# A Mamba block's scan loop and its output projection: C products in buffers of their own by state, last decays moved, a second projection group split, two low tiles on GpSimd

## The chip, the core and the metric

One core of one Trainium2 chip runs the whole program. The metric is the device time of one execution in microseconds (us); a run of this program has a median of 373.48 us over three runs (373.43 to 373.91). A core has TensorE (PE, matrix products; its weight loads are PEld), VectorE (DVE), ScalarE (ACT), GpSimd (POOL) and SyncE (SP, which here only issues DMAs). All of them run their own queue of instructions in order and wait for one another by semaphores.

## The reference, cut to what matters

Six blocks follow one another on x, 2 x 64 rows of 1024 values, each as x = x + block(layernorm(x)): a quantised product with a context, a Mamba block, a mixture of low-rank experts, a cross attention, a self attention with rotary positions, and a permuted MLP. The change lies in the second, where D = 2048 channels and N = 16 states:

```python
def step(state, xs):
    d_t, B_t, C_t, u_t = xs
    dA = jnp.exp(d_t[..., None] * A)
    state = dA * state + (d_t * u_t)[..., None] * B_t[:, None, :]
    y_t = jnp.einsum('bdn,bn->bd', state, C_t)
    return (state, y_t)
...
y = jnp.swapaxes(ys, 0, 1) + u * D_param
y = y * jax.nn.silu(gate)
return y @ W_out.T
```

## The kernel before

Time and batch (2 x 64 = 128) lie on the free axis, channels on the 128 partitions: 16 channel tiles k of 128. The 16 states are handled as two halves of 8 (HN), so the scan has 32 steps (STEPS): step s is channel tile s // 2, state half s % 2, a tile of 128 x 1024 values in the order (batch, state, time). Four steps make a quad (QUAD), which is two channel tiles; its y is gathered in one PSUM bank, y_bank(q). Every engine runs its own list of the steps, written out by hand:

- ScalarE: decay(s) (line 793, eight Exp of 128 x 126) makes dA; three buffers, so decay(s) waits for the scan of s - 3. In between stand the softplus parts, copies of the projection, the tanh of a gate group (gate_tanh, line 730), and DMA issues.
- TensorE: scan_input(s) (line 1138) puts the input of the scan into two PSUM banks; state_sum(s) (line 1180) sums the products over the states by accumulating transposes; fold_y(q) (line 1190) turns the sum back to channels on partitions and adds the two halves of a column block (ident2 is two identities on top of one another); turn (line 959) and gate tiles of W_in (line 1063) lie between. In iteration s of the loop at line 1193 the order is scan_input(s), turns, gate tile, state_sum(s - 3), fold.
- VectorE: scan(s) (line 1671) is one tensor_tensor_scan; then silu of a gate group (line 1609), copy_y(q) (line 1684, the y bank to h), skip_y(q) (line 1691, u * D added).
- GpSimd: the product of the state with C, in place (line 630), for steps 0 to 30; step 31 is on VectorE (times_c, line 1677). gate_y (line 621) multiplies a quad by its gate.

A state is in one of STATES = 4 buffers; scan(s) waits until state_sum(s - 4) has read that buffer.

Behind the loop comes the output projection, y @ W_out.T: 16 channel tiles in four groups (GD = 4 tiles), two halves nh of 512 output columns, eight units of W_out (1 MB each). Groups 0 and 1 are plain float32 products (output, line 1215, two passes for each). Groups 2 and 3 (GATE_HALF = 2 on) are split: ScalarE rounds unit m (high(m), line 820) and the left side (gated_high, line 810), VectorE takes the differences (low(m), line 1727; gated_low, line 1705), and split_products (lines 1002 and 1009) makes three products for each tile. There are three buffers for split units, so high(m) waits for the end of unit m - 3; two of the three lie over the scan's own buffers. gated_high(2) stands in ScalarE's loop at s = 30, between decays 30 and 31, since its left side needs the gate of quad 5, which GpSimd does behind product 30. The end of the projection is y_psum, 1 and 2: add_to_x (line 1482) adds the block's result to x, and the next block begins.

Weights come through a ring of 7 slots in the order of unit_list(). SP issues unit n when the unit before it in its slot is used up (last_use): for a split unit that is its low(m), for a plain one the product that reads it last. One slot more (x_wq 1) waits for y_psum 2.

## Time and profile before

| | |
|---|---|
| median of three runs | 373.48 us (373.43 to 373.91) |
| the profiled execution | 374.15 us, of which span 372.4 us |
| TensorE busy | 336.3 us (90%) |
| VectorE busy | 267.0 us (72%) |
| ScalarE busy | 206.0 us (55%) |
| GpSimd busy | 107.7 us (29%) |
| scan loop | about 84 to 184 us |
| mean granted TensorE clock | 0.989 |

The span is the time from the first to the last instruction; what is left of the execution's time lies around it. The granted clock is given as a share of TensorE's full speed. In a timeline a row is one instruction or several of the same kind back to back; its start counts from the start of the span, and what stands in brackets is how long the engine was idle before it and what ended that. Matmuls are pipelined: a row's length holds the tail of its last one, so the distance between the starts of two rows is the better measure of work.

### The profile page before, as it was taken

What the parts mean: (1) busy time and instruction counts of PE and PEld (TensorE: products, weight loads), DVE (VectorE), ACT (ScalarE), POOL (GpSimd) and SP (SyncE); (2) the same over time, 40 slices, a digit from 0 to 9 for tenths busy, and PEclk for the clock granted to TensorE, in tenths of its full rate; (3) what the DMA queues carried; (4) which work ended last, traced back from release to release, by engine and by line L of the source; (5) the groups of instructions that cost most, each with busy time, mean ns of one, the idle gap of its engine ahead of it and who ended that gap; (6) DMA issues with size and microseconds to landing.
All of it is one profiled execution on the core that took longest, in us unless ns stands there. A gap on an engine that the chain in (4) does not pass through costs nothing.

```text
span 372.4 us, 5061 instructions
## 1 busy us (share of the span) xinstructions
PE 336.3 (90%) x1928; PEld 215.4 (58%) x1928; DVE 267.0 (72%) x362; ACT 206.0 (55%) x402; POOL 107.7 (29%) x75
## 2 busy tenths in 40 slices
PE   0688999999899999999499999899999999899996
PEld 0334664653555555555165776687343577787795
DVE  2877887647979989886556698995721798975381
ACT  1985633189999999880702774463022468350350
POOL 2501000026988988888000020202000020300000
PEclk9999999999999999999699999999999999999999
DMA  6999999753030020661147799589999995000001
GB/s 243 423 422 419 420 325 422 283 212 113 2 110 6 0 113 3 225 243 46 57 127 271 285 396 400 215 329 352 393 429 363 427 422 236 2 2 2 0 2 56
DMA packets 12966, 81.85 MB, mean 220 GB/s; under 512 B 2109, under 2 KB 2365, under 8 KB 3661
## 3 DMA queue, kind: packets, MB, share of 16 engines
q1 hardware_dynamic: 11614, 78.23, 53.9%
q10 hardware_dynamic: 1296, 3.22, 2.3%
q8 instruction: 15, 0.25, 0.2%
q14 instruction: 9, 0.07, 0.1%
q0 software_dynamic: 32, 0.07, 0.1%
HBM read 80.86 MB, written 0.52 MB: 219 GB/s over the span
## 4 chain that ended last, share of the span: by engine, by line
PE 66%; DVE 17%; ACT 7%; DMA 6%; issue 2%; POOL 1%; SPq 0%; DVEq 0%; ACTq 0%
PE psum L1063 11%; PE psum L1002 8%; PE psum L1295 7%; PE psum L1138 7%; PE psum L1180 6%; DMA ring<-in_ctx 6%; PE psum L1215 4%; PE psum L1009 4%; PE psum L959 3%; DVE rounded L1727 3%; ACT arena L793 3%; PE psum L1414 2%; PE psum L1449 2%; PE psum L1190 2%; DVE arena L1671 2%
## 5 line engine op out<-in xcount | busy, mean ns | idle before, releaser
L793 ACT ACTIVATE arena<-arena 128x126 f32<-128x126 f32 x256 | 76.6, 394 | 3.2 <-DVE arena L1671 2.9
L1671 DVE TENSOR_TENSOR_SCAN arena<-arena,psum 128x1024 f32<-128x1024 f32 x24 | 54.6, 2281 | 5.8 <-PE psum L1138 5.0
L630 POOL TENSOR_TENSOR arena<-arena 128x1024 f32<-128x1024 f32 x23 | 54.3, 2365 | 8.4 <-DVE arena L1671 8.4
L571 POOL TENSOR_TENSOR small<-small 128x1 f32<-128x1 f32 x6 | 9.6, 1608 | 144.2 <-DVE small L1498 138.6
L1063 PE MATMUL psum<-ring,hT 128*128 128x512 f32 x104 | 50.2, 605 | 0.8 <-ACT hT L694 0.8
L1727 DVE TENSOR_TENSOR rounded<-ring,rounded 128x2048 fp32r<-128x2048 f32 x16 | 36.5, 2286 | 15.9 <-ACT rounded L820 15.9
L820 ACT ACTIVATE rounded<-ring 128x2048 fp32r<-128x2048 f32 x16 | 30.5, 1913 | 17.8 <-PE psum L1009 10.5
L1138 PE MATMUL psum<-plain 64*128 64x512 f32 x128 | 36.1, 641 | 0.4 <-DVE plain L1671 0.3
L1063 PEld LDWEIGHTS psum<-ring,hT 128*128 128x128 f32 x104 | 17.8, 190 | 21.9 <-issue 20.8
L1180 PEld LDWEIGHTS psum<-ident,arena 128*128 128x128 f32 x192 | 22.0, 141 | 11.7 <-issue 9.7
L1002 PE MATMUL psum<-rounded,split 128*128 128x512 f32 x96 | 24.7, 399 | 2.4 <-DVE rounded L1727 1.8
L1180 PE MATMUL psum<-ident,arena 128*128 128x128 f32 x192 | 25.2, 274 | 0.0
L1295 PE MATMUL psum<-ring,arena 128*64 128x512 f32 x96 | 24.4, 593 | 0.0
L1215 PE MATMUL psum<-ring,arena 128*128 128x512 f32 x32 | 16.9, 679 | 6.0 <-DVE arena L1609 6.0
L959 PE MATMUL psum<-ident,arena 128*128 128x128 f32 x120 | 18.7, 280 | 3.9 <-DVE arena L1649 1.5
L630 POOL TENSOR_TENSOR plain<-plain,arena 128x1024 f32<-128x1024 f32 x8 | 18.9, 2369 | 10.7 <-DVE plain L1671 10.7
L1002 PEld LDWEIGHTS psum<-rounded,split 128*128 128x128 f32 x96 | 17.5, 188 | 7.5 <-DVE rounded L1727 2.9
L959 PEld LDWEIGHTS psum<-ident,arena 128*128 128x128 f32 x120 | 13.4, 140 | 14.4 <-issue 8.7
L683 ACT ACTIVATE arena<-ring,small 128x2048 uint8<-128x2048 f32 (+1 forms) x9 | 16.9, 1900 | 7.9 <-DMA ring<-in_ctx 7.9
L959 PE MATMUL psum<-ident,h 128*128 128x128 f32 x48 | 7.4, 304 | 15.1 <-DVE h L1509 11.7
L1671 DVE TENSOR_TENSOR_SCAN plain<-arena,psum 128x1024 f32<-128x1024 f32 x8 | 18.2, 2277 | 2.5 <-PE psum L1138 2.4
L820 ACT ACTIVATE arena_halves<-ring 128x2048 fp32r<-128x2048 f32 x8 | 15.3, 1917 | 6.2 <-PE psum L1009 5.6
(237 smaller groups left out, 595.3 us busy)
## 6 DMA issues: line engine op xcount, KB each, us to landing
ring<-in_w_in SPq DMA_DIRECT2D x16, 1024.0 KB, 15.2
ring<-in_ctx SPq DMA_DIRECT2D x13, 1024.0 KB, 10.8
ring<-in_w_out SPq DMA_DIRECT2D x8, 1024.0 KB, 4.8
ring<-in_ctx_t SPq DMA_DIRECT2D x7, 1024.0 KB, 5.9
ring<-in_w_base SPq DMA_DIRECT2D x4, 1024.0 KB, 4.9
ring<-in_x_wk SPq DMA_DIRECT2D x4, 1024.0 KB, 9.8
ring<-in_a_wo SPq DMA_DIRECT2D x4, 1024.0 KB, 11.5
ring<-in_x_wq SPq DMA_DIRECT2D x3, 1024.0 KB, 9.0
```

What stands on the lines that cost most here:

```text
L630: pool.tensor_tensor(state[s % STATES], state[s % STATES], c, ALU.mult).then_inc(product_ready, 1)
L793: last = act.activation(to, of, ACT.Exp, scale=a_par[:, k, state_no:state_no + 1])
L820: act.activation(unit_halves[m % 3][:, 0, :, :], slot(split_units[m]), ACT.Copy).then_inc(unit_high, 1)
L959: last = pe.transpose(psum[:, bank, P * k:P * k + P], tile[:, c:c + P], ident[:, :])
L1002: pe.matmul(psum[:, bank, :], left(0, k0 + k), unit[:, w, k, :], start=(start and k == 0 and w == 0), stop=False)
L1063: last = pe.matmul(psum[:, proj_bank(j), :], hT[:, k, :], slot(w_in + u)[:, k % UK, :], **at)
L1138: last = pe.matmul(psum[:, input_bank(s, b), :], du[rows_of(b), left], bdiag[rows_of(b), right, :], start=True, stop=True)
L1180: last = pe.matmul(psum[:, y_bank(q), to:to + P], state[s % STATES][:, of:of + P], ident[:, :], start=(s % 2 == 0 and b == 0 and n == 0), ...
L1215: last = pe.matmul(psum[:, 4 + nh, :], sg[:, k, :], slot(u)[:, k % GD, :], start=(k == 0), stop=False)
L1295: last = pe.matmul(psum[L * b:L * b + L, bank, :], left[:, UK * kh + k, L * b:L * b + L], slot(u0 + b)[:, k, :], start=(kh == 0 and k == 0 ...
L1671: dve.tensor_tensor_scan(state[s % STATES], dA[:, s % 3, :], psum[:, p:p + 2, :].rearrange("p a b -> p (a b)"), 0.0, ALU.mult, ALU.add).th ...
L1727: dve.tensor_tensor(unit[:, 1, :, :], slot(split_units[m]), unit[:, 0, :, :].bitcast(F32), ALU.subtract).then_inc(unit_low, 1)
```

## The change

- state and product are apart: STATES = 3 state buffers and three product buffers. The product is written in the order (state, batch, time). scan(s) waits for the product of s - 3, the product of s waits for state_sum(s - 3).
- state_sum transposes 128 columns, one state of both batches, eight per step as before, all into the same 128 columns of y_bank; copy_y copies 256 columns, fold_y is two transposes.
- On ScalarE gated_high(2) is taken out of the loop, the last gate_tanh comes ahead of decay(31), and the load of bk goes behind product 30, because its place is now a state buffer.
- GATE_HALF = 1: group 1 of the output projection is split too. The low tiles of groups 1 and 2 are GpSimd's (behind its products), that of group 3 stays with VectorE. The order of W_out's units and all later numbers of split units (up by two) follow. On VectorE low(0) now comes first behind the loop.

```diff
-STATES = 4
+STATES = 3
-GATE_HALF = 2
+GATE_HALF = 1
-    units += [("w_out", i) for i in (0, 4, 1, 5, 2, 3, 6, 7)]
+    units += [("w_out", i) for i in (0, 4, 1, 2, 3, 5, 6, 7)]
...
-        state = [plain[:, 3 * HN * P:4 * HN * P]] + [carve(arena, 13408 + HN * P * i, HN * P) for i in range(STATES - 1)]
+        state = [carve(arena, 19040, HN * P), carve(arena, 23296, HN * P), plain[:, 3 * HN * P:4 * HN * P]]
+        product = [carve(arena, 13408 + HN * P * i, HN * P) for i in range(STATES)]
...
-        uses(None, None)
         for nh in range(2):
-            uses(None, (y_psum, nh + 1), split=True)
+            uses(None, None, (y_psum, nh + 1), split=True)
...
-                pool.tensor_tensor(state[s % STATES], state[s % STATES], c, ALU.mult).then_inc(product_ready, 1)
+                if s >= STATES:
+                    pool.wait_ge(reduced, s - STATES + 1)
+                pool.tensor_tensor(product[s % STATES].rearrange("p (n b t) -> p b n t", n=HN, b=B),
+                                   state[s % STATES].rearrange("p (b n t) -> p b n t", b=B, n=HN),
+                                   c.rearrange("p (b n t) -> p b n t", b=B, n=HN), ALU.mult).then_inc(product_ready, 1)
...
+            for g in range(GATE_HALF, 3):
+                pool.wait_ge(sg_high_ready, g - GATE_HALF + 1)
+                v = slice(GD * g, GD * g + GD)
+                pool.tensor_tensor(sg_low[:, v, :], sg[:, v, :], sg_high[:, v, :].bitcast(F32), ALU.subtract).then_inc(
+                    sg_low_ready, 1)
...
             for s in range(3, STEPS):
+                if s - 1 == GATE_AT[-1]:
+                    gate_tanh(NG - 1)
                 decay(s)
...
-                if s - 1 in GATE_AT:
+                if s - 1 in GATE_AT[:-1]:
                     gate_tanh(GATE_AT.index(s - 1))
...
-                if s == 30:
-                    gated_high(GATE_HALF)
...
-                    act.dma_start(bk, dram["bk"].to_broadcast([P, D])).then_inc(bias_in, 16)
...
             high(0)
+            gated_high(1)
+            gated_high(2)
...
             act.wait_ge(dbu_ready, STEPS)
-            act.wait_ge(reduced, STEPS - STATES + 1)
+            act.wait_ge(product_ready, STEPS - 1)
+            act.dma_start(bk, dram["bk"].to_broadcast([P, D])).then_inc(bias_in, 16)
             high(1)
+            act.wait_ge(reduced, STEPS)
+            high(2)
             gated_high(3)
-            for m in range(2, 7):
+            for m in range(3, 9):
                 high(m)
...
-                for b in range(B):
-                    to = 2 * P * (s // 2 % 2) + P * b
-                    for n in range(HN // 2):
-                        of = P * HN // 2 * b + P * n
-                        last = pe.matmul(psum[:, y_bank(q), to:to + P], state[s % STATES][:, of:of + P], ident[:, :],
-                                         start=(s % 2 == 0 and b == 0 and n == 0), stop=(s % 2 == 1 and n == HN // 2 - 1),
-                                         is_transpose=True, skip_group_check=True)
+                to = P * (s // 2 % 2)
+                for n in range(HN):
+                    last = pe.matmul(psum[:, y_bank(q), to:to + P], product[s % STATES][:, P * n:P * n + P], ident[:, :],
+                                     start=(s % 2 == 0 and n == 0), stop=(s % 2 == 1 and n == HN - 1), is_transpose=True,
+                                     skip_group_check=True)
...
-                for n in range(2 * B):
+                for n in range(2):
                     of = UN * (q % 2) + P * n
-                    last = pe.matmul(psum[:, y_bank(q), L * n:L * n + L], h[:, of:of + P], ident2, start=True, stop=True)
+                    last = pe.transpose(psum[:, y_bank(q), P * n:P * n + P], h[:, of:of + P], ident[:, :])
...
             for nh in range(2):
-                for k in range(GD, 2 * GD):
-                    output(nh, k)
-            for nh in range(2):
                 for g in range(GATE_HALF, NG):
...
-                    split_products(4 + nh, lambda a, k: (sg_low if a else sg_high)[:, k, :], 2 * nh + g - GATE_HALF, GD * g,
+                    split_products(4 + nh, lambda a, k: (sg_low if a else sg_high)[:, k, :], 3 * nh + g - GATE_HALF, GD * g,
...
                 if s >= STATES:
-                    dve.wait_ge(reduced, s - STATES + 1)
+                    dve.wait_ge(product_ready, s - STATES + 1)
...
-                dve.tensor_copy(h[:, UN * (q % 2):UN * (q % 2) + UN], psum[:, y_bank(q), :]).then_inc(y_copied, 1)
+                dve.tensor_copy(h[:, UN * (q % 2):UN * (q % 2) + 2 * P], psum[:, y_bank(q), 0:2 * P]).then_inc(y_copied, 1)
...
+            low(0)
             skip_y(STEPS // QUAD - 2)
             gate_y(STEPS // QUAD - 2)
-            gated_low(GATE_HALF)
+            low(1)
             copy_y(STEPS // QUAD - 1)
-            low(0)
             skip_y(STEPS // QUAD - 1)
             gate_y(STEPS // QUAD - 1)
-            low(1)
+            low(2)
             gated_low(3)
-            low(2)
-            low(3)
-            low(4)
+            for m in range(3, 7):
+                low(m)
```

## Rows read from the trace of the kernel before

**Rows 1.** Windows: us, busy us of each engine, granted clock, DMA share, GB/s.

```profile
125.00:150.00 25.00, 25.00 (x137) 14.64 (x138) 22.78 (x19) 23.93 (x80) 22.21 (x12) 1.00 0.12 43
...
180.00:185.00 5.00, 3.02 (x4) 1.50 (x5) 3.82 (x3) 4.72 (x6) 0.00 (x0) 0.50 0.26 103
...
235.00:240.00 5.00, 4.75 (x21) 3.86 (x21) 4.93 (x9) 2.29 (x3) 0.52 (x1) 1.00 0.26 79
```

**Rows 2.** TensorE's timeline in the loop: start us, length us, line, operation, count.

```profile
131.32 1.04 PE L1180 MATMUL psum<-ident,arena 128*128 128x128 f32 x8
132.19 1.00 PE L1190 MATMUL psum<-arena,h 128*128 128x64 f32 x8
133.13 1.13 PE L1138 MATMUL psum<-plain 64*128 64x512 f32 x4
```

**Rows 3.** Waits of VectorE from 96 to 175: us in total, times, longest.

```profile
DVE arena L1671 <- PE psum L1138: 5.0, 7, 1.2
```

**Rows 4.** GpSimd by line and form: count, busy us, mean ns of one.

```profile
L630 POOL TENSOR_TENSOR arena<-arena 128x1024 f32<-128x1024 f32 x23 | 54.3, 2365 | 8.4 <-DVE arena L1671 8.4
...
L653 POOL TENSOR_TENSOR arena<-arena,small 128x512 f32<-128x512 f32 x4 | 4.2, 1045 | 20.1 <-DVE small L1896 20.1
L614 POOL TENSOR_TENSOR arena<-arena 128x512 f32<-128x512 f32 x3 | 3.9, 1285 | 0.1
L594 POOL TENSOR_SCALAR x<-x,small 128x1024 f32<-128x1024 f32 x1 | 3.1, 3079 | 0.1
```

**Rows 5.** GpSimd's timeline behind product 30.

```profile
176.92 0.73 POOL L621 TENSOR_TENSOR arena<-arena 128x256 f32<-128x256 f32 x1
```

**Rows 6.** ScalarE's timeline at the loop's end, [idle before it, what ended that].

```profile
166.02 2.44 ACT L793 ACTIVATE arena<-arena 128x126 f32<-128x126 f32 x8
177.68 0.63 ACT L810 ACTIVATE arena_halves<-arena 128x512 fp32r<-128x512 f32 x1 [9.22 <-POOL arena L621]
...
180.54 0.57 ACT L730 ACTIVATE arena<-psum 128x512 f32<-128x512 f32 x1
181.01 1.90 ACT L820 ACTIVATE rounded<-ring 128x2048 fp32r<-128x2048 f32 x1
```

**Rows 7.** VectorE's timeline, one row of the loop, the others about its end.

```profile
130.26 0.67 DVE L1684 COPY h<-psum 128x512 f32<-128x512 f32 x1
...
172.25 2.28 DVE L1671 TENSOR_TENSOR_SCAN arena<-arena,psum 128x1024 f32<-128x1024 f32 x1
181.15 0.69 DVE L1609 SCALAR_TENSOR_TENSOR arena<-arena,psum 128x512 f32<-128x512 f32 x1 [6.61 <-ACT arena L730]
181.75 2.28 DVE L1671 TENSOR_TENSOR_SCAN arena<-arena,psum 128x1024 f32<-128x1024 f32 x1
184.06 1.23 DVE L1677 TENSOR_TENSOR arena<-arena 128x1024 f32<-128x1024 f32 x1
...
188.09 0.61 DVE L1691 SCALAR_TENSOR_TENSOR arena<-arena,small,psum 128x128 f32<-128x128 f32 x2 [2.20 <-PE psum L1190]
188.73 0.42 DVE L1699 TENSOR_TENSOR arena<-arena 128x256 f32<-128x256 f32 x1
```

**Rows 8.** TensorE's timeline, the first output products (three k tiles).

```profile
181.98 5.24 PE L1215 MATMUL psum<-ring,arena 128*128 128x512 f32 x6 [6.03 <-DVE arena L1609]
```

**Rows 9.** The chain that ended last: start us, length us, what, count.

```profile
194.94 6.92 PE psum L1215 x16
201.86 1.86 PE psum L1002 x8
203.72 0.93 PE psum L1009 x4
```

**Rows 10.** GpSimd's timeline, two of its one-element operations.

```profile
220.21 2.52 POOL L571 TENSOR_TENSOR small<-small 128x1 f32<-128x1 f32 x1 [42.56 <-DVE small L1498]
...
348.09 0.55 POOL L571 TENSOR_TENSOR small<-small 128x1 f32<-128x1 f32 x1 [21.68 <-DVE small L1498]
```

**Rows 11.** VectorE's timeline at the first of these two.

```profile
220.05 4.48 DVE L1727 TENSOR_TENSOR rounded<-ring,rounded 128x2048 fp32r<-128x2048 f32 x2
```

More of the change, by code:

```diff
@@ L1758, in _ @@
             center()
-            low_part(5, 0)
+            low_part(7, 0)
             left_low(2)
-            low_part(5, 1)
+            low_part(7, 1)
             variance(2)
-            low(6)
-            low(7)
+            low(8)
+            low(9)
             dve.wait_ge(bias_in, 48)
@@ L1787, in _ @@
                               ALU.mult).then_inc(g_ready, 1)
-            low(8)
+            low(10)
             dve.wait_ge(biased, 2)
@@ L1795, in _ @@
             center()
-            low_part(9, 0)
+            low_part(11, 0)
             left_low(4)
-            low_part(9, 1)
+            low_part(11, 1)
             variance(3)
-            low(10)
-            low(11)
+            low(12)
+            low(13)
             def query(nh):
@@ L1816, in _ @@
             query(0)
-            low(12)
+            low(14)
             query_low(0)
             query(1)
-            low(13)
-            low(14)
+            low(15)
+            low(16)
             query_low(1)
-            low(15)
+            low(17)
             dve.wait_ge(xk_psum, 2)
@@ L1847, in _ @@
                 if nh == 0:
-                    low(16)
+                    low(18)
                 dve.wait_ge(xatt_psum, nh + 1)
@@ L1853, in _ @@
             center()
-            low_part(17, 0)
+            low_part(19, 0)
             left_low(6)
-            low_part(17, 1)
+            low_part(19, 1)
             variance(4)
-            low(18)
+            low(20)
             step(dve.memset(vdup.rearrange("p b (h d) -> p (b h) d", d=DH + 1)[:, :, DH:], 1.0))
@@ L1871, in rotate @@
                 dve.tensor_tensor(to.rearrange("p (h d) -> p h d", h=heads), c, s, ALU.add).then_inc(signal, 1)
-            low(19)
+            low(21)
             dve.wait_ge(tables_in, 16)
@@ L1879, in _ @@
                 if n:
-                    low(21)
+                    low(23)
+                    low(24)
+                else:
                     low(22)
-                else:
-                    low(20)
                 dve.wait_ge(aq_psum, n + 1)
@@ L1887, in _ @@
                 rotate(psum[:, 7 if n else 1, :], H // 2, qrot[:, halves(n)], qrot_ready)
-            low(23)
+            low(25)
             dve.wait_ge(rstd_ready, 5)
@@ L1925, in _ @@
             divide(1)
-            low(24)
+            low(26)
             attn_low(1)
-            low(25)
+            low(27)
             for nh in range(2):
```

73 lines of the change are left out of this document (39 added, 34 removed).

## Prediction

> **What bounds the kernel now.** I read the windows first. Inside the scan loop TensorE is busy in all of 125 to 150 us, VectorE for 22.78 and ScalarE for 23.93 of the 25 [rows 1]. So I took TensorE's timeline over a few steps. Each step s issues the scan's input (line 1138, four matmuls), eight accumulating transposes of a product (line 1180) and mostly one gate tile; each fourth step also folds y (line 1190). The starts stand directly behind one another, so the engine's own work sets the pace: eight transposes take 0.87 us, and from a fold's start to the next input it is 0.94 [rows 2]. VectorE agrees: between 96 and 175 us its scans waited seven times, 5.0 us together, for that input, from scan 13 on; the longest, 1.2 us, is scan 17's [rows 3].
>
> Then the end of the loop. Scan 30 starts at 172.25, scan 31 only at 181.75 [rows 7]. Why: ScalarE did decays 30 at 166.02 (2.44 us), then stood 9.22 us in gated_high(2) [rows 6], which needs the gate that GpSimd does behind product 30, 0.73 us at 176.92 [rows 5]; only then came decays 31 and, at 180.54, the last tanh. The last silu, at 181.15 [rows 7], is what the first output product waited for: TensorE stood from 175.95 to 181.98, 6.03 us [rows 8], and came back at a granted clock of 0.50 [rows 1], which is the 1.2 GHz level; later it is at 2.4 GHz again. From there to about 213.1 (the end of the output projection: four split units of 1.86 + 0.93 = 2.8 us each from 201.86 on [rows 9]) TensorE has no gap. Everything later hangs on that moment.
>
> **The change part by part.** All times are on the old trace's axis.
>
> 1. *Products summed whole.* The state lies in the order (batch, state, time), the product now (state, batch, time), so that one transpose handles all 128 columns of one state. state_sum still has eight transposes: nothing saved. But y fills 256 columns instead of 512, and a fold is two transposes instead of eight passes. Price of two: at 0.87/8 each 0.22, and I take 0.28 for the start-up of so short a group. Saving 0.94 - 0.28 = 0.66 us per fold [rows 2]. copy_y halves too, from 0.67 to about 0.40 on VectorE [rows 7].
> How much of it counts? Not the fold of step 8: scan 9 waits for a tanh there. Of those of steps 12, 16, 20, 24 and 28 all do, if TensorE stays last. At step 17 two folds make it 1.32 earlier, against VectorE's 1.2 of waiting and about 0.7 that it gains itself (two half copies and a small wait): TensorE is still last. The 5.0 us of waiting and five half copies of 0.27 are more than five folds of 0.66. Sum 5 x 0.66 = 3.3; for friction with VectorE I take 3.2. ScalarE may run decays up to three steps ahead. Bounds: 0 (another engine takes over at once) and 3.3 + 0.7.
>
> 2. *New waits.* A scan waits for the product three steps back instead of the sum four back; a product waits for the sum three back. Queued behind a waiting scan are silu, copy_y and the next scan, behind a waiting product GpSimd's gates, and TensorE's sums wait for those. A product takes 2.365 [rows 4] and a step about 2.9, so the product three back is over some 3 us before it is needed. The sum three back ends before the scan of its step does (the input plus at most a gate tile and eight transposes, about 2.1 us, against the input plus a scan of 2.29). Margin 0.2 us or more: 0. If that margin goes, the product starts late by the difference, once a step.
>
> 3. *GpSimd's product with a permuted write.* No row shows one. The nearest: 128x512 with a broadcast operand in runs of 64 took 1.045 us, contiguous 1.285, so a three-dimensional read is not dearer; and upwards, the dearest 1024 columns of the engine, 3.08 for the scalar addition to x [rows 4]. I take 2.37 as before, the row nearest in kind. GpSimd then has 4 x 2.37 + 0.73 = 10.2 us per quad, where a quad of the new loop takes about 11.1: up to 2.6 us a product costs nothing, and cheaper is worth nothing.
>
> 4. *Last decays ahead.* gated_high(2) leaves the loop and the last tanh goes before decays 31. The turn that the tanh reads is queued on TensorE directly behind the input of scan 30, so it ends near 172; tanh 0.57 [rows 6], end near 172.7; decays 2.4, end near 175.0. Silu follows scan 30 at 174.5, 0.69; scan 31 runs from 175.1 to 177.4, its product of 1.23 to 178.7 [rows 7], the half copy to 179.1. What is late next for TensorE is the sum of product 29 (it ended before 174.6, and the sum of 28 is ahead of it): until 175.9, where TensorE's gap began. So output(0, 0) starts at 175.9 instead of 181.98: **6.1 us**. Without the gap I expect the full clock: the six passes of the first three products took 5.24 [rows 8], sixteen later ones 6.92 [rows 9], so six cost 2.6, and with 0.1 for the tail of the last this saves **2.5**. But fold 6 follows at 178.5 and needs the half copy of 179.1 and its semaphore: **0.7 lost**. The two last folds save 2 x 0.66 = **1.3**.
>
> 5. *Group 1 split.* Eight k tiles: 6.92 us plain, against two units of 2.8 [rows 9]: **1.3 saved**. Added are two ScalarE roundings of 1.90 [rows 6] and two VectorE differences of 2.24 (two took 4.48, [rows 11]). Covered? Fold 7 needs copy_y(7), now queued behind low(0), skip, gate and low(1): 179.1 + 2.25 + 0.6 + 0.4 [rows 7] + 2.25 = 184.6, with the copy 185.1. TensorE reaches that fold at 185.5: covered by 0.4. The six units then end at 188.5, 191.3, 194.1, 196.9, 199.7 and 202.5. A rounding waits for the end of the unit three before, and rounding and difference, 4.2 us, stand beside two units of 5.6: covered by 1.4. For the third unit skip, gate, low(2) and gated_low(3) end near 189.8, against 191.3: covered. Where this cover goes, each microsecond of VectorE is one of the total.
>
> 6. *Two low tiles on GpSimd*, 1.285 each [rows 4], ready near 179 and 180.5 and needed at 185.7 and 188.5. What they meet matters. GpSimd's one-element operation took 0.55 us at 348.09 but 2.52 at 220.21 [rows 10], where VectorE had begun a difference of two SBUF tensors 0.16 us earlier [rows 11]; it ended just behind that difference. So GpSimd is held by such VectorE work. Whether VectorE is held in turn no row shows: bounds 0 and all of the GpSimd work that meets it. If it is, VectorE's product of step 31 waits 0.2 for GpSimd's gate, low(0) about 1.0 for the first low tile, gate_y(6) 0.7 for the second; copy_y(7) ends near 187 and TensorE waits **1.5**. I take this value, since the hold seen lasted a whole instruction and most likely works both ways.
> The Trainium skill (SBUF — State Buffer, Who interferes with whom) states this lock for both directions; on the one that a row shows, the trace agrees with its 2.52 us. By that page the sum holds the 1.5, without it the sum is 1.5 more.
>
> 7. *DMA and queues.* The load of bk moves behind product 30 on ScalarE's queue, because its place is now a state buffer; its reader stands behind the two differences of 220.05 [rows 11], over 30 us later. SP's order of w_out follows the new use; the last one still waits for output(0, 3). The w_base loads wait for low tiles that come earlier. All later loads wait for releases that move with the work; at 235 to 240 the DMA engines had a share of 0.26 [rows 1], so the dense loading behind it is not backed up and moves too: 0.
>
> Sum: 3.2 + 6.1 + 2.5 - 0.7 + 1.3 + 1.3 = 13.7, less 1.5 for the hold: **12.2 us**. The profiled execution took 374.15 (span 372.4), so 361.95; the median of the runs, 373.48, lies 0.67 below it, which gives 361.3.
>
> **The rivals.**
> - *VectorE is not held by GpSimd:* 13.7 gained, 359.8. For: no row shows it held. Against: GpSimd is.
> - *The loop does not speed up*, because ScalarE (23.93 of 25 us) or VectorE is last as soon as TensorE gains: 3.2 less, 364.5. Against: VectorE's waits for inputs.
> - *The gain is given back downstream*, transfers becoming last behind 240 us. For: the dense loading there; against: the idle stretch before it. Half of the 12.2, about 367.4.
> - *The change does not do what it says:* scan 31 still late, say by a tanh held by its turn. Then loop, folds and split alone: 3.2 + 1.3 + 1.3 = 5.8, about 367.7.
> - *Slower: GpSimd's permuted product is dear.* It costs from 2.6 us on. A quad of 11.75 us now becomes 4X + 0.73; over six quads the tail's gain of 9 is gone at X = 3.1, just above the dearest row. At 3.3 the loop loses 13.1, and the time is about 377.5. For: nothing but the missing row.
> The Trainium skill (GPSIMD Engine Reference, Performance pitfalls for Q7 kernels) charges about half more for reads with an inner step over 8 bytes. The inner step stays at 4 bytes here, so by the page there is no charge; no row shows the charged case.
>
> **How the numbers follow.** Forecast 361.3 with 0.44; VectorE not held 0.27; loop not faster 0.14; downstream 0.05; change without effect 0.05; slower 0.03; and 0.02 for no change at all. The range of 359.0 to 365.0 takes in the first three, 0.85, with the 0.7 more that the loop may give. A measurement of this kernel tells 0.2% (0.75 us) from no change. Faster 0.95, same 0.02, slower 0.03.
>
> **What would show it.** Folds of two transposes, and some 11.1 us from fold to fold; scan 31 right behind the silu, near 172; no 6 us gap on TensorE and a granted clock of 1.00 throughout; the product at 2.37; VectorE's low(0) longer than 2.24 or late behind its copy, if the hold is real; the output projection's end near 201 instead of 213; the rest moved by one amount. I am wrong if the product takes over 2.6, if TensorE waits over 2 us for fold 7, or if the stretch behind the projection grows.

## The result, and the profile after

The changed kernel takes 361.20 us (median of four runs, 361.14 to 361.25) against 373.70 for the kernel before on the same chip (four runs, 373.43 to 374.41): a ratio of 0.9663, with a 95% interval of 0.9646 to 0.9679. The forecast was 361.3, its range 359.0 to 365.0. Of all the executions behind the medians of this document one is left out, the profiled one of the kernel without GpSimd's low tiles: it took 1129.9 us, where its four others took 360.6 to 360.7.

| | before | after |
|---|---|---|
| the profiled execution | 374.15 us | 361.25 us |
| its span | 372.4 us | 359.4 us |
| TensorE / VectorE busy | 336.3 / 267.0 us | 327.7 / 269.8 us |
| ScalarE / GpSimd busy | 206.0 / 107.7 us | 210.3 / 112.9 us |
| end of the output projection | 212.89 | 199.96 |
| from there to the end of the span | 159.5 | 159.4 |

The last two rows say where the gain lies: all 12.9 us of it ahead of the next block, and nothing given back behind. (The end is read at TensorE's idle products that follow the projection: line 965 before, line 979 after.)

The changed kernel's granted clock over the span in 40 slices, in tenths of full speed (9 stands for 90% or more):

```profile
PEclk9999999999999999999999999999999999999999
```

Windows of the changed kernel (us, busy us of PE, PEld, DVE, ACT and POOL, granted clock, DMA share, GB/s), to be held against [rows 1]:

```profile
125.00:150.00 25.00, 25.00 (x134) 13.85 (x133) 23.07 (x20) 24.90 (x84) 23.36 (x13) 1.00 0.16 53
180.00:185.00 5.00, 4.58 (x21) 2.94 (x20) 4.43 (x7) 2.45 (x2) 0.01 (x1) 1.00 0.71 256
```

In the loop TensorE is still full, and VectorE (23.07) and ScalarE (24.90) came nearer to it; ScalarE is now busy in all but 0.1 us of these 25. Behind the loop the granted clock is 1.00 where it was 0.50.

TensorE's timeline (start us, length us, line; idle time before it and what ended that), to be held against [rows 2] and [rows 8]:

```profile
130.65 1.04 PE L1192 MATMUL psum<-ident,arena 128*128 128x128 f32 x8
131.53 0.38 PE L1202 MATMUL psum<-ident,h 128*128 128x128 f32 x2
131.84 1.13 PE L1152 MATMUL psum<-plain 64*128 64x512 f32 x4
...
172.63 2.74 PE L1227 MATMUL psum<-ring,arena 128*128 128x512 f32 x6
175.99 0.44 PE L1202 MATMUL psum<-ident,h 128*128 128x128 f32 x2 [0.61 <-DVE h L1696]
...
182.89 0.44 PE L1202 MATMUL psum<-ident,h 128*128 128x128 f32 x2 [0.42 <-DVE h L1696]
183.08 2.11 PE L1016 MATMUL psum<-rounded,arena_halves 128*128 128x512 f32 x8
...
199.96 1.05 PE L979 MATMUL psum<-ident 128*128 128x128 f32 x8
```

A fold (now line 1202) takes 0.31 us from its start to the next input, instead of 0.94. The first output products start at 172.63, directly behind the sums, and six passes take 2.74 instead of 5.24. Two short waits are left, 0.61 and 0.42, each ahead of a fold, and each for VectorE's copy of y.

ScalarE's timeline, decays 31, to be held against [rows 6]:

```profile
169.50 2.42 ACT L803 ACTIVATE arena<-arena 128x126 f32<-128x126 f32 x8
```

VectorE's timeline over the end of the loop, to be held against [rows 7]:

```profile
169.10 2.28 DVE L1680 TENSOR_TENSOR_SCAN arena<-arena,psum 128x1024 f32<-128x1024 f32 x1
171.30 0.66 DVE L1618 SCALAR_TENSOR_TENSOR arena<-arena,psum 128x512 f32<-128x512 f32 x1
171.96 2.29 DVE L1680 TENSOR_TENSOR_SCAN arena<-arena,psum 128x1024 f32<-128x1024 f32 x1
174.28 1.32 DVE L1687 TENSOR_TENSOR arena<-arena 128x1024 f32<-128x1024 f32 x1
175.52 0.41 DVE L1696 COPY h<-psum 128x256 f32<-128x256 f32 x1
175.86 3.03 DVE L1741 TENSOR_TENSOR rounded<-ring,rounded 128x2048 fp32r<-128x2048 f32 x1
...
179.44 0.86 DVE L1712 TENSOR_TENSOR arena<-arena 128x256 f32<-128x256 f32 x1
180.22 2.28 DVE L1741 TENSOR_TENSOR rounded<-ring,rounded 128x2048 fp32r<-128x2048 f32 x1
```

Scan 30 starts at 169.10, which is 3.15 earlier than before, and scan 31 directly behind the last silu, at 171.96. Then two rows are longer than their work: low(0) at 175.86 (3.03, the next one of the same form 2.28) and gate_y(6) at 179.44 (0.86, against 0.42 in [rows 7]). GpSimd is what they meet. Its rows by line and form, and its timeline there:

```profile
L632 POOL TENSOR_TENSOR arena<-arena 128x1024 f32<-128x1024 f32 x21 | 49.4, 2361 | 15.0 <-DVE arena L1680 14.8
...
L645 POOL TENSOR_TENSOR arena_halves<-arena,arena_halves 128x512 fp32r<-128x512 f32 x2 | 5.5, 2786 | 0.0
```

```profile
174.48 5.53 POOL L645 TENSOR_TENSOR arena_halves<-arena,arena_halves 128x512 fp32r<-128x512 f32 x2
```

The product with its permuted write (line 632) costs 2.361 on average, against 2.365 contiguous [rows 4]. The two low tiles (line 645) took 5.53 together, where two contiguous subtractions or products of this size take 2 x 1.285 [rows 4]. Put in a row, the numbers fit two engines that let each other pass one instruction at a time: tile 1 waits for product 31, low(0) for tile 1, tile 2 for low(0), and gate_y(6) for tile 2, which ends at 180.01.

### The profile page after: what moved, and what is told of

Same layout as the page of the kernel before. It is cut to its first block, busy times and chain, and to the rows that moved or that the text cites. A ratio compares the mean times of both kernels' runs of the same rounds, so it can differ in the third digit from the quotient of the medians.

```text
span 359.4 us, 5024 instructions
## 1 busy us (share of the span) xinstructions
PE 327.7 (91%) x1888; PEld 210.1 (58%) x1888; DVE 269.8 (75%) x363; ACT 210.3 (59%) x405; POOL 112.9 (31%) x77
## 4 chain that ended last, share of the span: by engine, by line
PE 58%; DVE 20%; ACT 11%; DMA 6%; issue 3%; POOL 0%; SPq 0%; DVEq 0%; ACTq 0%
PE psum L1077 11%; PE psum L1016 9%; PE psum L1304 8%; DMA ring<-in_ctx 6%; ACT arena L803 6%; PE psum L1152 5%; PE psum L1023 5%; PE psum L1192 4%; PE psum L973 3%; DVE rounded L1741 3%; DVE arena L1680 2%; PE psum L1423 2%; PE psum L1458 2%; DVE arena_halves L1741 2%; DVE rounded L1749 1%
## 5 line engine op out<-in xcount | busy, mean ns | idle before, releaser
L632 POOL TENSOR_TENSOR arena<-arena 128x1024 f32<-128x1024 f32 x21 | 49.4, 2361 | 15.0 <-DVE arena L1680 14.8
L1680 DVE TENSOR_TENSOR_SCAN arena<-arena,psum 128x1024 f32<-128x1024 f32 x22 | 49.9, 2278 | 4.8 <-PE psum L1152 3.1
L830 ACT ACTIVATE rounded<-ring 128x2048 fp32r<-128x2048 f32 x18 | 34.5, 1917 | 20.0 <-PE psum L1023 10.4
L1192 PEld LDWEIGHTS psum<-ident,arena 128*128 128x128 f32 x256 | 28.9, 141 | 16.8 <-issue 14.8
L1192 PE MATMUL psum<-ident,arena 128*128 128x128 f32 x256 | 33.6, 275 | 0.0
L1016 PE MATMUL psum<-rounded,split 128*128 128x512 f32 x104 | 26.6, 398 | 1.4 <-ACT split L701 0.7
L1680 DVE TENSOR_TENSOR_SCAN plain<-arena,psum 128x1024 f32<-128x1024 f32 x10 | 22.8, 2278 | 1.6 <-PE psum L1152 1.3
L632 POOL TENSOR_TENSOR arena<-plain,arena 128x1024 f32<-128x1024 f32 x10 | 23.6, 2359 | 1.3 <-DVE plain L1680 1.2
L973 PE MATMUL psum<-ident,arena 128*128 128x128 f32 x120 | 18.7, 280 | 4.5 <-DVE arena L1658 1.5
L1016 PEld LDWEIGHTS psum<-rounded,split 128*128 128x128 f32 x104 | 19.0, 188 | 6.4 <-ACT split L701 1.7
L973 PEld LDWEIGHTS psum<-ident,arena 128*128 128x128 f32 x120 | 13.4, 140 | 14.9 <-issue 9.3
L973 PE MATMUL psum<-ident,h 128*128 128x128 f32 x48 | 7.4, 304 | 15.0 <-DVE h L1518 11.6
L1741 DVE TENSOR_TENSOR arena_halves<-ring,arena_halves 128x2048 fp32r<-128x2048 f32 x8 | 18.3, 2285 | 0.8 <-ACT arena_halves L830 0.8
## 6 DMA issues: line engine op xcount, KB each, us to landing
ring<-in_a_wo SPq DMA_DIRECT2D x4, 1024.0 KB, 11.6
```

Of the source, the lines that this page charges most:

```text
L632: pool.tensor_tensor(product[s % STATES].rearrange("p (n b t) -> p b n t", n=HN, b=B), state[s % STATES].rearrange("p (b n t) -> p b n t", ...
L830: act.activation(unit_halves[m % 3][:, 0, :, :], slot(split_units[m]), ACT.Copy).then_inc(unit_high, 1)
L973: last = pe.transpose(psum[:, bank, P * k:P * k + P], tile[:, c:c + P], ident[:, :])
L1016: pe.matmul(psum[:, bank, :], left(0, k0 + k), unit[:, w, k, :], start=(start and k == 0 and w == 0), stop=False)
L1192: last = pe.matmul(psum[:, y_bank(q), to:to + P], product[s % STATES][:, P * n:P * n + P], ident[:, :], start=(s % 2 == 0 and n == 0), sto ...
L1680: dve.tensor_tensor_scan(state[s % STATES], dA[:, s % 3, :], psum[:, p:p + 2, :].rearrange("p a b -> p (a b)"), 0.0, ALU.mult, ALU.add).th ...
```

## The experiments

The theory was the prediction's sum: products by state, the decays moved ahead and the split are three gains that add, because TensorE is last everywhere, less a hold of VectorE by GpSimd. All times are medians; "saved" is against the kernel before as it was measured beside each. Those medians lie between 373.70 and 374.18, so a difference of some 0.3 us between two changed kernels is no more than that scatter, unless rows show where it arises; the ratios, which take the scatter out in part, are given for this.

### Do the parts add?

Decays ahead alone. The last tanh goes ahead of decays 31, gated_high(2) behind high(0); gate_y on VectorE waits for GpSimd's gate before it, and the rest is the kernel before.

```diff
             for s in range(3, STEPS):
+                if s - 1 == GATE_AT[-1]:
+                    gate_tanh(NG - 1)
                 decay(s)
...
-                if s - 1 in GATE_AT:
+                if s - 1 in GATE_AT[:-1]:
...
-                if s == 30:
-                    gated_high(GATE_HALF)
...
             high(0)
+            gated_high(GATE_HALF)
```

> The kernel before with one part of the change: gated_high(2) behind high(0), the last tanh ahead of decays 31, and VectorE's gate waiting for GpSimd's. Theory A (my sum): the 6.0 us gap of TensorE and the 2.5 us of slow clock go, and fold 6 then waits some 1.0 us for a full copy_y(6); 7.5 us saved, 366.2. Rival B: the clock falls elsewhere, or the gap only moves to another wait; 6 saved or less, 367.7 and up.

Measured: 366.60 us (366.55 to 366.67), ratio 0.9809 (0.9794 to 0.9823), 7.3 saved. TensorE's timeline of it:

```profile
175.75 2.74 PE L1216 MATMUL psum<-ring,arena 128*128 128x512 f32 x6
179.38 1.10 PE L1191 MATMUL psum<-arena,h 128*128 128x64 f32 x8 [0.89 <-DVE h L1685]
```

Output(0, 0) follows the sums at 175.75, within 0.2 of the 175.9 that the prediction read from the place where the gap began. The six passes run at once in 2.74. Fold 6 waits 0.89, since the copy of y is still a whole bank here.

Products by state alone. Three state and three product buffers, the sums, copies and folds of the changed kernel, and the load of bk moved, as the buffers need; decays, projection and units as before.

```diff
-STATES = 4
+STATES = 3
...
-                pool.tensor_tensor(state[s % STATES], state[s % STATES], c, ALU.mult).then_inc(product_ready, 1)
+                if s >= STATES:
+                    pool.wait_ge(reduced, s - STATES + 1)
+                pool.tensor_tensor(product[s % STATES].rearrange("p (n b t) -> p b n t", n=HN, b=B),
...
-                for n in range(2 * B):
+                for n in range(2):
                     of = UN * (q % 2) + P * n
-                    last = pe.matmul(psum[:, y_bank(q), L * n:L * n + L], h[:, of:of + P], ident2, start=True, stop=True)
+                    last = pe.transpose(psum[:, y_bank(q), P * n:P * n + P], h[:, of:of + P], ident[:, :])
```

> The kernel before with the other part: products by state in own buffers, half copies, folds of two transposes (the load of bk moved, which the buffers need). Theory A: 3.15 us in the loop and 2 x 0.63 for the last two folds, scan 31 still stalled by decays 31 as before: 4.4 saved, 369.3. Rival B: the fold's saving is hidden behind other engines when alone, or the stall takes it; 373.7.

Measured: 369.71 us (369.44 to 370.22), ratio 0.9893 (0.9878 to 0.9908), 4.2 saved. TensorE's timeline of it:

```profile
178.87 5.35 PE L1219 MATMUL psum<-ring,arena 128*128 128x512 f32 x6 [6.03 <-DVE arena L1613]
```

The whole block of work came 3.1 earlier (178.87 against 181.98), and the gap of 6.03 with the slow passes behind it (5.35) is untouched. The loop's gain and the gap are two separate things.

Both, without the split: GATE_HALF and the order of the units stay as before, and the low tile of group 2 stays with VectorE.

> Both parts together, group 1 of the projection plain and the low tile of group 2 on VectorE as before. Theory A: the parts add, and the changed kernel has only 1.3 for the split units less 0.4 for the wait of fold 7 on top: 362.0 to 362.1. Rival B: the split and GpSimd's tiles bring the whole 1.3, 362.5. Rival C: they bring nothing, 361.2.

Measured: 361.95 us (361.85 to 361.96), ratio 0.9683 (0.9667 to 0.9699), 12.0 saved. Singly the two saved 7.3 + 4.2 = 11.5. They add, and 0.3 of what is over is the shorter wait of fold 6. TensorE's timeline of it, the two folds behind the loop:

```profile
176.05 0.44 PE L1195 MATMUL psum<-ident,h 128*128 128x128 f32 x2 [0.62 <-DVE h L1692]
...
182.37 0.38 PE L1195 MATMUL psum<-ident,h 128*128 128x128 f32 x2
```

Here fold 7 has no wait. So of the changed kernel's 361.20 the split accounts for 0.75 only: its own 1.3, less about 0.6 for the wait of fold 7 that came with it.

The changed kernel with the decays' part undone: the tanh behind decays 31, gated_high(1) and (2) between decays 30 and 31.

```diff
-                if s - 1 == GATE_AT[-1]:
-                    gate_tanh(NG - 1)
                 decay(s)
...
-                if s - 1 in GATE_AT[:-1]:
+                if s - 1 in GATE_AT:
...
+                if s == 30:
+                    gated_high(1)
+                    gated_high(2)
...
             high(0)
-            gated_high(1)
-            gated_high(2)
```

> The changed kernel with the decays part undone: gated_high(1) and (2) in the loop at s = 30, the last tanh behind decays 31. Theory A: TensorE's gap of 6 us and the slow clock come back (6.1 + 2.5), while the waits of fold 6 (0.6) and fold 7 (0.4) go: 368.8. Rival B: the decays part is worth only the gap, 366.3 to 367.

Measured: 368.25 us (367.78 to 368.62), ratio 0.9852 (0.9836 to 0.9868), 7.05 more than the changed kernel, where the same part alone saved 7.3. Its windows and TensorE's row behind the gap:

```profile
180.00:185.00 5.00, 5.00 (x18) 2.68 (x17) 4.96 (x6) 1.91 (x1) 0.00 (x0) 0.75 0.56 196
```

```profile
178.87 4.59 PE L1226 MATMUL psum<-ring,arena 128*128 128x512 f32 x6 [6.04 <-DVE arena L1617]
```

The gap is back (6.04), and with it a granted clock of 0.75 in 180 to 185. Here the six passes took 4.59, not 5.24: what the clock costs behind the gap varied between 1.9 and 2.6 us in the three kernels that have it (passes of 4.59, 5.24 and 5.35, at a mean granted clock of 0.60, 0.52 and 0.50, against 2.74).

### Does GpSimd hold VectorE, and what does it cost?

The question is whether the two take turns, in both directions, when both read two operands from SBUF, or only GpSimd waits. First the price in this kernel. GpSimd's low tiles are taken away; ScalarE writes them as zeros instead, so the low part of two groups is missing from the product.

```diff
-            for g in range(GATE_HALF, 3):
-                pool.wait_ge(sg_high_ready, g - GATE_HALF + 1)
...
             high(1)
+            act.wait_ge(sg_high_ready, 2)
+            for g in range(GATE_HALF, 3):
+                v = slice(GD * g, GD * g + GD)
+                act.activation(sg_low[:, v, :], sg[:, v, :], ACT.Copy, scale=0.0).then_inc(sg_low_ready, 1)
```

> The changed kernel without GpSimd's two low tiles: ScalarE writes zeros in their place while it is idle behind high(1), so the low part of groups 1 and 2 is left out of the result. Theory A: VectorE's low(0), product 31 and gate_y(6) return to 2.28, 1.23 and 0.42, and only the 0.42 us that TensorE waited for fold 7 counts: 360.8. Rival B: the hold costs the 1.5 of the prediction: 359.7. Rival C: the longer VectorE instructions have another cause than GpSimd: they stay, 361.2.

Measured: 360.65 us (four runs, 360.58 to 360.67), ratio 0.9642 (0.9628 to 0.9656): 0.55 below the changed kernel by the medians, 0.8 by the ratios. No rows of this kernel are used, so only its times speak. The hold costs 0.55 to 0.8 us: more than the 0.4 of the expectation's theory A, but nearer to it than to the 1.5 of its rival B, and rival C (nothing) is out.

The mechanism by itself: four stages appended behind the end of the changed kernel, with four 128 x 1024 additions on each engine. Stage 1: first GpSimd alone, then VectorE alone. Stage 2: both at once. Stage 3: both at once, VectorE's second operand in PSUM. Stage 4: VectorE as in stage 2, GpSimd only writes (memset).

```diff
+                for n in range(4):
+                    last = dve.tensor_tensor(ring[:, 2 + n // 2, D * (n % 2):D * (n % 2) + D], left, right, ALU.add)
...
+                for n in range(4):
+                    to = ring[:, 4 + n // 2, D * (n % 2):D * (n % 2) + D]
+                    last = pool.memset(to, 0.0) if only_write else pool.tensor_tensor(to, left, right, ALU.add)
```

> The changed kernel with four stages behind its last addition, each of four 128x1024 additions on an engine: GpSimd alone, VectorE alone (two SBUF inputs), both at once, GpSimd with VectorE reading PSUM as the second input, and GpSimd only writing (memset) with VectorE reading two SBUF tensors. Theory A (each holds the other for whole instructions): alone 1.22 (VectorE) and about 2.36 (GpSimd); together a pair takes 3.6 and both look longer. Rival B (only GpSimd is held): VectorE stays at 1.22, GpSimd starts after VectorE's four. Rival C: both are slowed a little, by shared reading. By all of them PSUM as second input and the memset change nothing.

Measured: 400.64 us with the four stages, in a single execution. VectorE's timeline, stages 1 to 4, then the first two instructions of stage 2 singly, then GpSimd's:

```profile
366.36 4.63 DVE L2001 TENSOR_TENSOR ring<-ring 128x1024 f32<-128x1024 f32 x4 [9.34 <-POOL ring L674]
371.19 11.06 DVE L2001 TENSOR_TENSOR ring<-ring 128x1024 f32<-128x1024 f32 x4 [0.20 <-POOL small L678]
384.48 4.62 DVE L2001 TENSOR_TENSOR ring<-ring,psum 128x1024 f32<-128x1024 f32 x4 [2.23 <-POOL ring L674]
393.91 4.63 DVE L2001 TENSOR_TENSOR ring<-ring 128x1024 f32<-128x1024 f32 x4 [4.82 <-POOL ring L674]
```

```profile
371.19 1.22 DVE L2001 TENSOR_TENSOR ring<-ring 128x1024 f32<-128x1024 f32 x1 [0.20 <-POOL small L678]
372.33 3.36 DVE L2001 TENSOR_TENSOR ring<-ring 128x1024 f32<-128x1024 f32 x1
```

```profile
357.09 9.23 POOL L674 TENSOR_TENSOR ring<-ring 128x1024 f32<-128x1024 f32 x4 [21.38 <-DVE small L2003]
...
371.30 13.15 POOL L674 TENSOR_TENSOR ring<-ring 128x1024 f32<-128x1024 f32 x4
384.61 9.27 POOL L674 TENSOR_TENSOR ring<-ring 128x1024 f32<-128x1024 f32 x4 [0.17 <-POOL ring L674]
```

Alone the four take 4.63 on VectorE (1.16 each) and 9.23 on GpSimd (2.31 each). Together they took 11.06 and 13.15. If each lets the other pass after every instruction, with VectorE first, VectorE ends after 4 x 1.16 + 3 x 2.31 = 11.6 and GpSimd after 4.63 + 9.23 = 13.9: measured 11.1 and 13.3 from the first start. So both are held. The single rows show the turns themselves: VectorE's first addition takes 1.22, and each of the other three 3.35 or 3.36, its own work and one addition of GpSimd. Had the two shared the reading evenly, VectorE would have ended after some 9.3 (an estimate, twice 4.63). With one operand in PSUM nobody is held (4.62 and 9.27), nor is VectorE by a memset (stage 4: 4.63). That is the expectation's theory A. It fits the loop, where the scans, which read PSUM, took 2.28 beside GpSimd's products throughout.

The Trainium skill (SBUF — State Buffer, Who interferes with whom) states the lock for both directions; the stage with both at once agrees, with 13.3 us against 13.9 for one after the other.

The kernel with the late decays shows the same from the other side. There the same two tiles ran while VectorE stood idle (171.42 to 178.03) and took 2.50 together instead of 5.53, and low(0), which came after them, took 2.28:

```profile
174.49 2.50 POOL L645 TENSOR_TENSOR arena_halves<-arena,arena_halves 128x512 fp32r<-128x512 f32 x2
```

Is the help of GpSimd worth anything then? The low tiles of groups 1 and 2 go to VectorE, behind low(0) and low(1):

```diff
             low(0)
+            gated_low(1)
             skip_y(STEPS // QUAD - 2)
             gate_y(STEPS // QUAD - 2)
             low(1)
+            gated_low(2)
             copy_y(STEPS // QUAD - 1)
```

> The changed kernel with the two low tiles of groups 1 and 2 on VectorE (0.68 each, ahead of copy_y(7)) instead of GpSimd. Theory A: GpSimd's help is worth almost nothing, since it lengthens VectorE's work by 1.2 us where the tiles themselves take 1.36: 361.3 to 361.5. Rival B: GpSimd's tiles are free, so this costs the whole 1.36: 362.5.

Measured: 361.52 us (five runs, 361.36 to 361.55), ratio 0.9665 (0.9650 to 0.9679). VectorE's timeline:

```profile
175.92 2.28 DVE L1734 TENSOR_TENSOR rounded<-ring,rounded 128x2048 fp32r<-128x2048 f32 x1
178.12 0.68 DVE L1712 TENSOR_TENSOR arena_halves<-arena,arena_halves 128x512 fp32r<-128x512 f32 x1
```

low(0) is back at 2.28, which shows that GpSimd's tiles were what lengthened it, but VectorE does two tiles of 0.68 itself. (Product 31 still takes 1.33: that 0.1 comes from GpSimd's gate ahead of it, 173.86 to 174.58, and not from the tiles.) That is 1.36 of its own work against 1.2 of being held, and fold 7 waits 0.44 against 0.42. The two low tiles on GpSimd are worth 0.3 us by the medians and nothing by the ratios.

### What is left of the waits

The waits for folds 6 and 7 come from the order on VectorE (the copy of y behind product 31, or behind low(1)). Copy_y(6) goes ahead of scan 31, copy_y(7) behind low(0), and on TensorE the last sum directly behind the one before, fold 7 two products earlier:

```diff
             state_sum(STEPS - 2)
+            state_sum(STEPS - 1)
             output(0, 3)
             output(1, 0)
             output(1, 1)
-            state_sum(STEPS - 1)
+            fold_y(STEPS // QUAD - 1)
             output(1, 2)
             output(1, 3)
-            fold_y(STEPS // QUAD - 1)
...
+                if s == STEPS - 2:
+                    copy_y(STEPS // QUAD - 2)
...
             low(0)
+            copy_y(STEPS // QUAD - 1)
             skip_y(STEPS // QUAD - 2)
             gate_y(STEPS // QUAD - 2)
             low(1)
-            copy_y(STEPS // QUAD - 1)
```

> The changed kernel with copy_y(6) ahead of scan 31, the last state sum directly behind the one before, copy_y(7) directly behind low(0), and fold 7 two output products earlier. Theory A: TensorE is last everywhere in the projection but for its waits of 0.61 (fold 6) and 0.42 (fold 7); both go, 360.2. Rival B: the unit differences queued behind the copies become late and take the gain back, 361.2 or more.

Measured: 360.60 us (360.49 to 360.68), ratio 0.9641 (0.9627 to 0.9655): 0.6 below the changed kernel, 0.4 short of what was expected. VectorE's rows of product 31 and low(0), GpSimd's of the two low tiles, TensorE's of the last sum:

```profile
174.64 2.32 DVE L1687 TENSOR_TENSOR arena<-arena 128x1024 f32<-128x1024 f32 x1
176.88 3.36 DVE L1743 TENSOR_TENSOR rounded<-ring,rounded 128x2048 fp32r<-128x2048 f32 x1
```

```profile
174.61 3.48 POOL L645 TENSOR_TENSOR arena_halves<-arena,arena_halves 128x512 fp32r<-128x512 f32 x2
```

```profile
177.02 1.09 PE L1192 MATMUL psum<-ident,arena 128*128 128x128 f32 x8 [0.43 <-DVE arena L1687]
```

Both waits for folds are gone. Neither theory named what came instead: the copy ahead of scan 31 moved product 31 from 174.28 to 174.64, to just behind the start of GpSimd's first tile (174.61): now product 31 is the one that waits, 2.32 for work of 1.23, and low(0), with 3.36, waits for the second tile. TensorE waits 0.43 for that product, which is the 0.4 that was missed. Which side was held hung on a copy of 0.4 us.

Hence the last version: this order, and the low tiles on VectorE, behind copy_y(7) and low(1), so that nothing on GpSimd meets product 31.

```diff
             low(0)
             copy_y(STEPS // QUAD - 1)
+            gated_low(1)
             skip_y(STEPS // QUAD - 2)
             gate_y(STEPS // QUAD - 2)
             low(1)
+            gated_low(2)
             skip_y(STEPS // QUAD - 1)
```

> e7_sum_early with the low tiles of groups 1 and 2 on VectorE, behind copy_y(7) and behind low(1), and nothing of GpSimd beside VectorE's differences. In e7 product 31 took 2.32 us beside GpSimd's tile and the last state sum waited 0.43 us for it. Theory A (that hold is what is left of TensorE's waits): 360.2. Rival B: VectorE's added 1.36 us makes the third unit's differences late (it has some 0.3 to spare), 360.6 or more.

Measured: 359.90 us (five runs, 359.86 to 360.01), ratio 0.9625 (0.9611 to 0.9639), the fastest of all, 1.3 below the changed kernel. VectorE's product 31 and low(0), TensorE's rows from the first output on:

```profile
174.54 1.23 DVE L1681 TENSOR_TENSOR arena<-arena 128x1024 f32<-128x1024 f32 x1
175.68 2.28 DVE L1736 TENSOR_TENSOR rounded<-ring,rounded 128x2048 fp32r<-128x2048 f32 x1
```

```profile
172.65 2.74 PE L1221 MATMUL psum<-ring,arena 128*128 128x512 f32 x6
175.23 0.38 PE L1196 MATMUL psum<-ident,h 128*128 128x128 f32 x2
...
198.44 1.05 PE L973 MATMUL psum<-ident 128*128 128x128 f32 x8
```

Product 31 takes 1.23 and TensorE has no gap from 172.65 to 198.44, where the projection ends 1.5 earlier than in the changed kernel. It came out 0.3 below the 360.2 expected: that number counted the idle times before the two folds (0.61 and 0.42), while from start to start the waits had cost 0.78 and 0.58.

### The rival that would have made it slower

From what price does GpSimd's product decide? The prediction said from 2.6 us a product, with the gain gone at 3.1. An extra product of 128 x 256 (0.76 us on average, its result unused) stands behind each of GpSimd's products from step 8 on:

```diff
+                if s >= 8:
+                    pool.wait_ge(const_zero, s - 6)
+                    pool.tensor_tensor(spare_out, cwide[:, 0:2 * P], cwide[:, 2 * P:4 * P], ALU.mult).then_inc(const_zero, 1)
```

> The changed kernel in which GpSimd makes one more product of 128x256 (0.73 us, into an unused place) behind each product from step 8 on, so that a step costs it about 3.1 us. Theory A (the room I gave GpSimd, up to 2.6 us a product): a quad takes 4 x 3.07 + 0.73 = 13.0 instead of 11.1, over 5.7 quads 10.8 us, less about 1 that GpSimd has idle at the start: about 371. Rival B: at 3.1 us the whole gain is gone as the slower rival said, 373.7. Rival C: GpSimd has room for 0.7 us more a step: 361 to 363.

Measured: 375.07 us (six runs, 373.52 to 375.38), ratio 1.0007 (0.9981 to 1.0032): the gain is gone, as the rival said, but not by its working alone. GpSimd's timeline at the end of the loop, and the rows of product 31 on VectorE and of the first output product and fold 6 on TensorE:

```profile
180.61 0.82 POOL L638 TENSOR_TENSOR arena<-arena 128x256 f32<-128x256 f32 x1
...
184.29 0.81 POOL L622 TENSOR_TENSOR arena<-arena 128x256 f32<-128x256 f32 x1
184.97 2.58 POOL L649 TENSOR_TENSOR arena_halves<-arena,arena_halves 128x512 fp32r<-128x512 f32 x2
```

```profile
180.19 8.44 DVE L1691 TENSOR_TENSOR arena<-arena 128x1024 f32<-128x1024 f32 x1
```

```profile
181.72 2.74 PE L1231 MATMUL psum<-ring,arena 128*128 128x512 f32 x6
189.02 0.44 PE L1206 MATMUL psum<-ident,h 128*128 128x128 f32 x2 [4.56 <-DVE h L1700]
```

From 115 us on GpSimd is never idle in the loop, a step costs it 3.00 us from start to start instead of the 3.1 aimed at, and its gate of quad 5 starts at 184.29, against 173.80 in the changed kernel, 10.5 us later. TensorE's first output product comes 9.1 later (181.72 against 172.63), where theory A had some 9.8 for the loop. The rest of the 13.9 arose behind it. Product 31 on VectorE, work of 1.23, took 8.44: it stood until GpSimd's chain ended (188.63 - 1.23 = 187.4, against 184.97 + 2.58 = 187.55), past all of its six instructions from 180.61 on, not one. So fold 6 waited 4.56, 3.9 longer than in the changed kernel, and behind it the sum took 1.35 from start to start instead of 0.88 and the six passes 3.95 instead of 2.74, 1.7 together; fold 7 no longer waited, which gives 0.6 back. This was seen in one profiled execution; why VectorE got no turn here, while it did in the four-stage probe, no run settles.

The same with an extra product of 128 x 16, 0.22 us:

> The changed kernel with one more product of 128x16 on GpSimd behind each product from step 8 on, so small that a step costs it about 2.7 us. Theory A (2.6 us a product are free, TensorE is last until then): GpSimd's quad is 4 x 2.7 + 0.73 = 11.5 against 11.1 to 11.3; 0 to 1.5 us more than the changed kernel, 361.2 to 362.7. Rival B: GpSimd is already as late as TensorE, and each added 0.3 counts over 23 steps: 368.

Measured: 361.41 us (361.39 to 361.46), ratio 0.9665 (0.9651 to 0.9678), 0.2 more than the changed kernel. GpSimd's timeline in the loop:

```profile
168.99 2.36 POOL L633 TENSOR_TENSOR arena<-plain,arena 128x1024 f32<-128x1024 f32 x1
171.31 0.22 POOL L638 TENSOR_TENSOR arena<-arena 128x16 f32<-128x16 f32 x1
171.49 2.37 POOL L633 TENSOR_TENSOR arena<-arena 128x1024 f32<-128x1024 f32 x1
```

From product to product it is 2.50 here where GpSimd is not idle between them, against 2.32 in the changed kernel (166.46 to 168.78), and TensorE's first output product starts at 172.66, against 172.63. So 0.18 us more a step is covered, which fits the bound of 2.6 but does not reach it; at what price between 2.50 and 3.00 a step GpSimd begins to decide, no run shows. The 0.2 arises at product 31: behind GpSimd's gate, which now comes 0.2 later, it took 1.51, against 1.32 in the changed kernel, and fold 6 waited 0.80 instead of 0.61.

## Why the prediction held, point by point

The terms, with the measured ones from start to start on TensorE's two timelines. They add up to 212.89 - 199.96 = 12.93.

| term | predicted | measured |
|---|---|---|
| loop, up to scan 30 | 3.2 | 3.15 (172.25 to 169.10) |
| output(0, 0) behind scan 30 | 6.1 | 6.20 (9.73 to 3.53) |
| six passes at the full clock | 2.5 | 2.49 |
| wait for fold 6 | -0.7 | -0.78 |
| the last two folds | 1.3 | 1.22 |
| group 1 split | 1.3 | 1.23 |
| wait for fold 7 (the hold) | -1.5 | -0.58 |
| sum | 12.2 | 12.9 |

- *Products summed whole.* Right in size and in its reason. A quad took 10.8 to 11.3 us from fold to fold, but for the first (11.8); 11.1 was named. The price of a short fold was taken at 0.28 and was 0.31. Near its end the loop now hangs on VectorE too: scans 29 to 31 follow one another there with only a skip or a silu between them, and in the middle ScalarE is busy for 24.90 of 25 us. So a further cut on TensorE alone would most likely not bring its full size; no run tries it.
- *New waits.* Right: from 96 to 175 TensorE waits twice, 0.56 us for a silu and 0.35 for a scan, both before 118 (0.32 in all before the change), and never for a product; scan 31 and product 31 follow directly.
- *Permuted write.* Right: 2.361 against the 2.37 taken. The two experiments with added work show that the cover was real but less than 0.7 us a step, and that a product dearer by that would have taken 9.1 of the 12.9 by itself, and with the held product 31 behind it all of them.
- *Decays ahead.* Right. It is the largest part: 7.3 alone, 7.05 when taken out of the whole. About a third of it is not the gap but the slow clock behind it.
- *Split.* Its own 1.3 was right. The cover of 0.4 for fold 7 was not enough, as said, once VectorE is held.
- *The hold, the mis-sized term.* The step that failed is "low(0) about 1.0 for the first low tile, gate_y(6) 0.7 for the second; copy_y(7) ends near 187 and TensorE waits 1.5". The mechanism is the one shown above; its size was off. VectorE lost 0.75 on low(0), 0.44 on gate_y(6) and 0.1 on product 31, which makes 1.3 instead of 1.9. The cover in front of fold 7 was larger by the rest: without the hold the copy would have ended near 181.5, 0.9 ahead of TensorE (182.5), not 0.4. So the wait is 0.4 to 0.6 instead of 1.5.
- *From the profiled execution to the median.* The second miss, with the other sign: a correction of 0.67 was taken off, what lay between the profiled execution and the median before. After the change it was 0.05 (361.25 to 361.20), and before, against the four runs made beside the changed kernel (373.70), 0.45. Such a distance belongs to the one execution, not to the kernel. By the profiled executions the gain was 12.9 and the forecast 0.7 too small; this and the 0.6 cancel, and that is why 361.3 met 361.20. The agreement to 0.1 is luck, the agreement to 1 us is not.
- *The rivals.* VectorE not held (359.8) falls by the probe and by its rows; the loop not faster by the 3.15; a gain given back downstream by the 159.5 and 159.4; no effect by scan 31. The slower one did not occur; at 3.0 us a step the gain is indeed gone, but of the 13.9 us above the changed kernel only 9.1 came from the loop, and the rest, 3.9 for the wait of fold 6 and 1.7 for the slow clock less 0.6 at fold 7, from the held product 31, which the rival's working didn't have.

## What to carry to other kernels

A wait for another engine that stands in an in-order queue ahead of work on the critical path costs its own length and, when it is long (6 us here, while waits of up to 1.9 us had no such price), the slow clock behind the gap: look at each engine's list for such a wait before cutting work. Where one engine is last everywhere, gains that are costed on its own timeline add up almost to the tenth; where a step hands work to GpSimd, look first at what VectorE does at that moment, since here an operation with two SBUF operands there made both of them wait. Such work is better put beside VectorE operations that read PSUM, or kept on VectorE when it costs as much as the hold.

## What the runs showed of the hardware

- GpSimd and VectorE, each with two operands in SBUF, take turns by instruction: 13.3 us together against 13.9 in series, and 3.35 us for a VectorE addition of 1.16 beside one of GpSimd's of 2.31. One operand in PSUM, or a memset on GpSimd, lifts it.
- The turn is not assured. Behind a dense chain on GpSimd one VectorE product of 1.23 us took 8.44.
- A three-dimensional write in runs of 64 elements costs GpSimd nothing: 2.361 against 2.365 us for 128 x 1024 elements.
- A gap of 6 us on TensorE was followed by six passes at a mean granted clock of 0.50 to 0.60, at a price of 1.9 to 2.6 us; one of 4.56 by a mean of 0.63 to 0.68 and a price of 1.7 (0.5 in the sum, 1.2 in the six passes). Gaps of 0.4 to 0.9 us had no such price, nor had one of 1.91 in the kernel with the dear product, whose six passes behind it took 2.74.
